# Self-attention: where TensorE makes the output projection of the tile two back

## The reference, cut to what matters

```
q, k, v = heads(x @ Wqkv)
attn = softmax(q @ k.T * 16 ** -0.5)       # inside one sequence: 32 x 32 per head
out = (attn @ v) @ Wout * sigmoid(x @ Wgate)
blended = ls1 * ((1 - alpha) * ssm_out + alpha * out)
```

## Time and profile before

| | |
|---|---|
| median of 3 runs | 1111.95 us (1110.38 to 1117.57) |
| profiled execution | 1117.38 us, its span 1115.6 us |
| PE busy in the span | 1001.6 us, 90% |
| mean granted TensorE clock | 0.947 of full speed |
| self-attention's first matmul, last ScalarE operation | at 520.7 us, at 629.3 us of the span |

### The profile page before, as it was taken

How to read it: one execution, slowest core, us unless ns; L and a number is a source line. 1 busy time by engine, 2 the same in 40 slices (tenths; PEclk the granted TensorE clock), 3 DMA queues, 4 the chain that set the end, 5 groups by cost and what they waited for, 6 DMA issues and landing times. The chain is left out here.

```text
span 1115.6 us, 29608 instructions
## 1 busy us (share of the span) xinstructions
PE 1001.6 (90%) x10648; PEld 876.1 (79%) x10648; DVE 782.6 (70%) x2304; ACT 619.3 (56%) x1356; POOL 654.2 (59%) x806
## 2 busy tenths in 40 slices
PE   5899999999999998898999628999999628999998
PEld 3699999999999986687888527887878516988997
DVE  7477777777777776655566589776667486777884
ACT  2466666766666651633455486666656364444541
POOL 1388787777877881344666317767776213655443
PEclk9899999999999998899999859999999767999999
DMA  5222122322223222890000511333333348556501
GB/s 164 62 68 62 60 64 82 84 59 63 64 78 87 59 52 84 216 372 9 4 3 4 95 71 35 52 54 49 52 55 48 95 161 273 131 139 172 127 7 11
DMA packets 68636, 95.51 MB, mean 86 GB/s; under 512 B 12764, under 2 KB 48048, under 8 KB 68496
## 3 DMA queue, kind: packets, MB, share of 16 engines
q1 hardware_dynamic: 52464, 73.02, 21.0%
q0 software_dynamic: 16032, 20.62, 11.2%
HBM read 73.68 MB, written 22.18 MB: 86 GB/s over the span
## 5 line engine op out<-in xcount | busy, mean ns | idle before, releaser
L1898 POOL DMA_INDIRECT e_x<-rows,source x71 | 75.7, 1066 | 99.2 <-ACTq L1735 34.4
L695 DVE TENSOR_SCALAR xa_pT<-xa_ptp 128x512 f32<-128x512 f32 x128 | 88.1, 688 | 56.3 <-PE xa_ptp L490 56.3
L127 POOL TENSOR_TENSOR xa_cs<-xa_ctx,xa_cs 128x514 fp32r<-128x514 f32 x64 | 82.7, 1293 | 76.3 <-ACT xa_cs L634 75.3
L640 ACT ACTIVATE xa_pr<-xa_pr,xa_nm 128x257 f32<-128x257 f32 x256 | 108.7, 498 | 3.1 <-DVE xa_nm L691 3.1
L1909 POOL DMA_INDIRECT out_x<-e_y,target x32 | 53.8, 1682 | 74.3 <-DVE e_y L2686 63.2
L684 DVE TENSOR_SCALAR_CACHE_REDUCE xa_pr<-xa_sc 128x257 f32<-128x257 f32 x256 | 93.6, 423 | 0.0
L2523 PE MATMUL e_hb<-e_xTs,e_w1s 128*128 128x512 f32 x384 | 91.7, 399 | 1.9 <-issue 1.9
L1903 POOL DMA_INDIRECT base<-e_y,place x39 | 71.3, 1829 | 37.1 <-DVE e_y L2181 18.7
L2577 ACT ACTIVATE e_h<-e_hb,rc_F_b 128x512 f32<-128x512 f32 x64 | 44.1, 689 | 87.5 <-PE e_hb L2523 86.8
L2539 PE MATMUL e_yb<-e_w2s,e_hTs 128*128 128x256 f32 x768 | 89.1, 277 | 0.0
L2539 PEld LDWEIGHTS e_yb<-e_w2s,e_hTs 128*128 128x128 f32 x768 | 87.8, 188 | 0.1
(11 more groups left out here) (360 smaller groups left out, 2903.3 us busy)
## 6 DMA issues: line engine op xcount, KB each, us to landing
e_w<-in_F_W SPq DMA_DIRECT2D x16, 1024.0 KB
w<-in_W SPq DMA_DIRECT2D x24, 512.0 KB, 10.0
xa_ctx<-in_ctxT SPq DMA_DIRECT2D x32, 257.0 KB, 3.3
xa_ctx<-in_ctxT SPq DMA_DIRECT2D x64, 128.5 KB, 3.6
xa_vb<-vlx SPq DMA_DIRECT2D x64, 128.0 KB
rows<-xs_oT SPq DMA_DIRECT2D x4, 516.0 KB, 9.7
xs_oT<-in_x SPq DMA_DIRECT2D x4, 512.0 KB, 4.6
base<-xs_oT SPq DMA_DIRECT2D x4, 512.0 KB, 3.1
```

The lines of the kernel that those rows point to most:

```text
L127: pool.tensor_tensor(o["cs"][:, par, 1, :, 0:S], o["ctx"][:, slot, :, par, :], o["cs"][:, par, 0, :, 0:S], ALU.subtract).then_inc(o["cr_re ...
L640: act.activation(pr[:, par, g, :], pr[:, par, g, :], ACT.Exp, bias=nm[:, par, g:g + 1], scale=-1.0).then_inc(exp_ready, 1)
L695: dve.tensor_scalar(pT[:, par, 2 * h:2 * h + 2].rearrange("p g t c -> p (g t c)"), ptp[:], 1.0, None, ALU.min).then_inc(pT_ready, 1)
L1898: return pool.indirect_dma_start(out=out, out_offset=None, in_=rows, in_offset=bass.IndirectOffsetOnAxis(ap=index, axis=0))
```

## The change

The block that makes the output projection of tile t-2 is moved, with its two waits and its signal, from behind the products for v to right behind the products for q and k, ahead of the wait for `k_ready` and of the turns. Nothing is added or removed, and no other engine's list changes.

```
@@ -1301,6 +1301,13 @@
                             mm = pe.matmul(qkb[:, c, :], wqk[:, k, P * c:P * c + P],
                                            nT[:, k, bass.ds((t + 1) * P, P)], start=(k == 0), stop=(k == 1))
                     mm.then_inc(qk_ready, 1)
+                if there(t, 2):
+                    pe.wait_ge(oT_stored, t - 1)
+                    if there(t, 3):
+                        pe.wait_ge(a1_ready, t - 2)
+                    for k in range(2):
+                        mm = pe.matmul(outb[:, 0:D], oT[:, k, :], wout[:, k, :], start=(k == 0), stop=(k == 1))
+                    mm.then_inc(out_ready, 1)
                 if there(t, 0):
                     pe.wait_ge(k_ready, t * 4 + 4)
                 if there(t, 1):
@@ -1331,13 +1338,6 @@
                                                start=(k == 0 and b == 0), stop=(k == 1 and b == 3),
                                                skip_group_check=True)
                     mm.then_inc(v_ready, 1)
-                if there(t, 2):
-                    pe.wait_ge(oT_stored, t - 1)
-                    if there(t, 3):
-                        pe.wait_ge(a1_ready, t - 2)
-                    for k in range(2):
-                        mm = pe.matmul(outb[:, 0:D], oT[:, k, :], wout[:, k, :], start=(k == 0), stop=(k == 1))
-                    mm.then_inc(out_ready, 1)
                 if there(t, 1):
                     pe.wait_ge(pT_stored, t)
                     pe.wait_ge(va_placed, t * 3)
```

## The result

The changed kernel takes 1118.07 us in the median of 20 runs (1114.03 to 1124.28), the kernel before 1114.82 in the median of its 20 (1110.38 to 1117.57). The ratio is 1.0036, with a 95% interval of 1.0022 to 1.0050: a loss of 4.0 us (2.5 to 5.6), small and clear of noise. (The two medians alone differ by 3.25.) The three runs shown ahead of the prediction had their median 2.9 us under that of the twenty.

A forecast was written before the change was run, and what follows sets the result against it. TensorE, without idle time in the middle, bounds the kernel; its groups' sum sets the 6.16 us period. Middle 0 plus end 1.0 gives 1.0 us, taking the median from 1111.95 to 1113.0; range 1109.8 to 1118.0.

The forecast's parts named there:

- its class, within 1%: Whole kernel: time stays within 1% of before, chance 0.93, against 0.02 for faster and 0.05 for slower.
- The groups are the same and so is their sum: Middle periods: TensorE's groups keep their cost in the new order, period stays 6.16 us, cost 0.
- a bound of 0 below and 3.0 above: Eleven middle periods: no gain possible; at most 0.27 us more each, 3.0 us, if oT's release is slow.
- The start: Step 2: projection fills the gap ahead of the turns; step 3's q and k 0.65 us earlier, scores 0.41 behind.
- The wait for oT: Rival, middle: with 0.02 us to spare the wait binds in each tile, up to 0.27 us per period; chance 0.25.
- pulling weight loads ahead: Middle: a projection waiting for oT would show its first load, 0.19 us each, 2.1 us over eleven periods.
- The end: Steps 15 and 16: projection ahead of the turns delays the chain; last projection 1.04 us late, same slow groups.
- step 15 slow as well: Upper bound at the end: low clock already takes step 15's projection, turns and scores, 1.5 us more, 2.5 late.
- rule on oscillation: Clock rival, middle: recurring gaps lower the clock, period some 10.5 us, 47 us over eleven; chance 0.05 including like mishaps.

The follow-up runs named there:

- e9: Changed kernel plus a useless product as long as the projection, in the projection's old place between v and the probabilities times v; 1123.45 us, one run.
- e11: Kernel before plus useless products for q and k on TensorE in steps 15 and 16, ahead of the wait for the keys; ratio 0.9987.
- e7: Projection at a third place, behind the probabilities times v at the step's end, in all steps; ratio 1.0028.
- e6: Changed kernel with 32 more long met waits on TensorE in step 1, shifting later instructions by 32 places; ratio 1.0049.
- e10: Kernel before with 32 more long met waits on TensorE in step 1; 1113.10 us, one run.
- e5: Changed kernel plus useless products for q and k in steps 15 and 16, ahead of the projection's wait; ratio 1.0019.
- e4: Kernel before with the projection's new place in steps 15 and 16 alone; ratio 0.9995.
- e1: Kernel before once more, unchanged, for a second profile; 1115.14 us in one run.
- e2: Changed kernel once more, unchanged, against the kernel before; ratio 1.0027.

## Why the prediction was wrong

The median came out at 1118.07, 0.07 over the range, the shift at 4.0 us instead of 1.0. Its sign and its class, within 1%, were right. By its own steps:

**"The groups are the same and so is their sum": failed both ways.** A group's cost depends on its neighbours. The projection costs 0.87 us between q and k and the turns (e9), and 1.06 between v and the probabilities times v. With one of these neighbours of each kind it costs 0.96: in step 16 of e11 it stands between the turns and the probabilities times v (618.79 to 619.75), in e7 between the latter and q and k. The weight loads of the latter show it, in the kernel before:

```profile
552.38 1.01 PEld L1350 LDWEIGHTS sa_otb<-sa_pT,sa_vbd 128*64 128x64 f32 x32 [0.33 <-issue]
```

and in the changed kernel, where they follow v's:

```profile
550.12 1.01 PEld L1350 LDWEIGHTS sa_otb<-sa_pT,sa_vbd 128*64 128x64 f32 x32
```

Behind the projection (128*128) the first load of the other shape (128*64) came after 0.33 us of idleness; behind v's loads it follows at once. But v's shape (128*32) is another one too, so a difference in shape is not enough. That the change of shape is the cause is argued, not shown; no run was made for it alone. Over eleven periods at 6.05 it gains 1.2 us. Against it stand the breaks: 68.73 less eleven times 6.05 is 2.2 us. Net 0.8 in the mean of the two profiles, where I had 0 and a bound of 0 below and 3.0 above.

**What the breaks are.** Each ends 2.4 to 2.7 us after a packet of 16 KB has started in the instruction queue. For the break that ends at 563.79, the window from 561.30 to 563.90 has this in it and nothing else (each digit is a fortieth of the window, 0.065 us):

```profile
DMA  0800000000000000000000000000000000000000
...
q8 instruction: 1, 0.02, 2.1%
```

The packet starts near 561.4. TensorE needs instructions faster where they are short: v is 128 instructions, loads included, in 1.03 us, the projection eight in 1.06.

The places of the breaks can be counted. The phase has 340 matmuls ahead of step 2 and 152 in each step from there on, so 10 of 32 in step 2 is behind the 470th; the others are behind the 1,098th (step 6), 1,223rd (7), 1,851st (11) and 1,977th (12). The distances are 5, 1, 5 and 1 times 125 or 126, each matmul with a weight load of its own. In e7, with another order, the counts are 470, 1,223, 1,851 and 1,976; in e6 462, 1,090, 1,216 and 1,843. So something ends every 125.6 matmuls, whatever the order of the groups, and it makes TensorE wait where it falls into the last of v or into the probabilities times v right behind it. In the kernel before, the same counts lie behind 10, 30, 3 and 23 of the 32 as well, without a break, since TensorE arrives there a projection later.

The one of step 2 in detail: in the kernel before a packet started near 537.83, as v began, and by 540.2, 2.4 us later, TensorE was still within the first ten of the short products behind the projection, which began at 540.06. So the projection, in its old place, covered the fetch; e6, e7, e9 and e10 all agree, and the moved group's second service is the term that my sum lacked. The Trainium skill ("Advanced Engine Details and Errata", section ISA Cache) gives an instruction cache of 32 KB, 128 KB on TensorE, with lines of 16 KB, which are 256 instructions, and says "Only 2 cache lines!". The trace agrees in the size of the packet, and in the distance: 125.6 matmuls with their loads are 251 instructions, which by my estimate leaves five for the waits. How many lines there are no run here shows.

**The start.** The gap ahead of the turns in step 2 was filled, as predicted, by the projection at 534.21. What it gave went to the first break, in the same step: the probabilities times v took 1.92 us there (537.24 to 539.16) instead of 1.05, and the start 20.39 against 20.42. In the mean the start gave nothing.

**The wait for oT** binds, by 0.08 us and not by 0.27. In the periods right behind a break, where oT is early, the projection costs 0.87 in the changed kernel too (565.91 to 566.78). The Trainium skill's rule ("TensorE: Matmul & The Clock Gate", section on what each phase of a matmul is for) on pulling weight loads ahead, which one that waits for oT cannot be, would have made it 0.19, my estimate from the earlier trace rows; the trace has less than half. As a rival it was right in direction and small in effect, since the shorter neighbour more than paid for it.

**The end: right mechanism, wrong size.** Measured from step 14's q and k, I had 1.04 + 0.65 = 1.7 us more; the profiles have 3.2 (the mean of 20.83, 20.53 and the shifted 20.94, less that of 17.87, 18.57 and the shifted 16.38). At full clock the two orders take 17.87 (e5) and 16.38 (e11): the chain's share is 1.5 us, near my 1.7, which had the same slow groups on both sides. The rest, 1.7, is the clock, a difference that I had put at 0, and this is the term that was too small: the clock costs the changed kernel 2.9 on average, in steps 15 and 16, and the kernel before 0 to 2.2. I had taken the low clock from the one profile that I had, where it fell in step 16 only, and kept the case "step 15 slow as well", 1.5 more, as a bound. It was the case in all three profiles of the changed order: its idle time in step 15 is 1.8 us, in e4 with 0.74 it did not happen. In the kernel before, the same 1.52 us of idleness ahead of step 15's turns was followed by a projection of 1.07 us in the first profile (617.81 to 618.88) and of 1.78 in e1 (615.39 to 617.17). The Trainium skill's rule on oscillation (the same page, section on HAM oscillation), that gaps between bursts bring the clock down each time, thus holds at the pipeline's end for the changed order, but not in every profile of the old one; in the middle, with gaps of up to 0.85 us, the clock stayed at 1.00.

Together: start 0, middle 0.8, end 3.2, so 4.0 us, which is the measured shift. That it fits so closely is in part luck: the end of the old order alone varies by 2.2 us between profiles, and the second measurement (e2) gave 3.0 us. As for the range: the time shown ahead was the median of three runs, and of the 5.1 us between my 1113.0 and 1118.07, 2.9 are the distance of that median from the one of twenty. Without it 1118.07 would have lain in the range; the shift would have been as wrong.

## What to carry to other kernels

A group that is moved takes two things along that no busy time shows: what it costs beside its neighbour, and what it hides, be it a switch of shape or the fetch of the next instructions. Look for long runs of very short instructions that the move brings together. Where a pipeline empties, find the chain and ask what is put ahead of it; and take the clock's effect there from more than one profile, since it jumps between runs of the same program.

## What the runs showed of the hardware

- TensorE can run out of instructions: in code with 64 short matmuls (16 ns from one to the next, each with its own weight load) followed directly by 32 more (33 ns), it stood still for 0.17 to 0.85 us about once in three steps, at places 125.6 matmuls or five times that apart, with "issue" as the releaser and a 16 KB packet of the instruction queue started 2.2 to 2.8 us before the end of the break.
- The same matmuls of 256 columns cost 0.87, 0.96 or 1.06 us for four, depending on what stands ahead of them and behind them.
- Useless matmuls of 1.60 and 2.05 us, put into two gaps, kept the 2.4 GHz level, and took 2.9 us off a chain that was 20.8 long.
